# Ends of two mixture-of-experts stages taken in single token blocks, and the loads of the stages after them moved past the block end

## Chip, cores and metric

The kernel is one program on one core of one Trainium2 chip. The metric is the device time of one execution in microseconds (us); less is better. PE is TensorE, PEld its weight load, DVE VectorE, ACT ScalarE, POOL GpSimd, SP the sync engine that only issues transfers. A name with q (SPq, POOLq) is that engine's sequencer.

## What is computed

The reference runs four layers on x of shape 2 x 1024 x 256, T = 2048 rows in all. Two parts matter here, layer 1's top-2 experts with the attention block that follows, and layer 2's experts that choose tokens with the attention that follows:

```python
# layer 1, feed-forward: every token goes to its 2 best of 8 experts
for eid in range(e):
    w = jnp.sum(jnp.where(idx == eid, vals, jnp.zeros((), x.dtype)), axis=-1)
    h = jax.nn.gelu(x_flat @ w1[eid].T, approximate=False)
    y = h @ w2[eid].T
    out = out + w[:, None] * y
# layer 2, attention block: self attention, context attention, feed-forward, each under a layer norm
y = layernorm(y + sa, g1, beta1)
y = layernorm(y + ca, g2, beta2)
y = layernorm(y + ff, g3, beta3)
# layer 2, feed-forward: each of 8 experts takes its 1024 best tokens
h = jax.nn.silu(jnp.einsum('ecd,edh->ech', routed, w1)) * jnp.einsum('ecd,edh->ech', routed, w3)
routed_out = jnp.einsum('ech,ehd->ecd', h, w2).reshape(-1, dim)
out = jnp.zeros_like(xt).at[token_idx].add(routed_out)
# layer 3, attention: queries from the rows, keys and values from the context of 77 rows
out = jnp.einsum('bhqk,bhkd->bhqd', weights, vh)
```

## The kernel before, in words

The rows x stay on chip as 16 token blocks of 128 rows (`k.x`). `program` runs stages one after another; each stage is one `nc.Block()`, in which each engine has its own list of instructions, written out by hand, and only semaphores order the engines. A block ends when every engine has reached its end (each passes a DRAIN there); then `Semaphores.clear` clears the stage's semaphores and all engines meet once more (L790, L791). Only then does the next stage's first instruction start.

**`top2_experts` (tiles with t_).** 23 tiles (TILES) of 256 token slots, sorted by expert. For tile j PE turns the gathered rows, multiplies them by w1 (layer1), and, one tile later, by w2 (layer2); a product of float32 precision is three matmuls (`split_matmul`, L798 to L800). layer2 puts two token blocks of 128 (u = 0, 1) side by side in one PSUM bank and signals `y_psum` once for both. DVE scales both with the gates in one instruction (`scaled`, L1395), and POOL adds them to the DRAM tensor `t_total` with two indirect DMAs (`add`, L1276). POOL starts tile j's adds only when tile j-1's have landed, since two adds to one row must not be in flight together. At the end SP waits for all adds and issues eight loads of the sum back into x (L1261), signalled by `k.x_back`; they need not have landed at the block's end.

**`transformer_block` (tb_).** SP loads `tb_after`, eight columns `tb_turned`, then `tb_affine`, the context rows and the weights. PE begins with 28 filler matmuls (`keep_busy`, L1419) that compute nothing and stand there for the clock; then it waits for the first normalised rows. DVE takes the first statistics (`first_moments`, L2127) once `x_back[0]` has been signalled.

**`choice_experts` (ch_).** 16 groups s (8 experts x 2 turns) of four token blocks. PE's order is layer1(s), turn(s+1), layer2(s-1); each layer2 is 48 matmuls in two halves of two token blocks, each half in its own bank. layer2 waits at its start for all four parts of `ch_hid_lo`. DVE copies each half (`take_output`, L2832) and POOL adds it to `ch_total` with two indirect DMAs (`add`, L2645). At the end SP waits until all adds have landed.

**`narrow_attention` with tag L3_ (tiles L_).** SP loads x back from `ch_total` in four groups, the first two ahead of the weights and biases of keys and values. PE's list is keys (L3452), values (L3459), the turned rows of group 0 (L3444), queries (L3481), ... and, once keys and values are placed, the first scores (L3493). DVE's list is: statistics and normalising of token blocks 0 to 7 (L3305, L3662), the keys into their block-diagonal place (`L_kbd`, L3695), statistics of blocks 8 to 15, values (L3670), four more blocks normalised, values again, the mask (L3714), and then `take` of the first scores (L3723).

The lines that begin DVE's list in that attention:

```python
statistics(range(0, NT // 2))
normalise(range(0, NT // 2))
constants(dve)
...
dve.wait_ge(kv_loaded, 64)
dve.wait_ge(keys_psum, 1)
```

## Time and profile before

| what | value |
|---|---|
| runs of the kernel before | 1691.48, 1693.34, 1696.11 us; median 1693.34 |
| the profiled execution | 1693.98 us, its span 1692.2 us |
| busy share of the span | PE 85%, PEld 71%, DVE 65%, ACT 45%, POOL 38% |
| top-2 stage ends, transformer block begins | 789 us into the span |
| choice stage ends, last attention begins | 1458 us into the span |
| granted TensorE clock, mean | 0.93 |

Times are counted from the span's start. In a timeline row the first number is the start and the second the length of a run of equal instructions; the bracket at the end says how long the engine had sat idle and what released it. The order in which instructions stand is shown below as the built programs have it; no time is in those rows.

### The profile page before, as it was taken

To read this page: it belongs to the slowest core of one execution; us is meant where nothing else is said; L and a number is where in the kernel's file an instruction comes from. 1 tells how busy PE (TensorE), PEld (TensorE's weight loads), DVE (VectorE), ACT (ScalarE), POOL (GpSimd) and SP (SyncE) were. 2 spreads that over 40 slices of the span, in tenths; PEclk is the share of its full clock that TensorE was granted. 3 is DMA by queue.
4 is the path that set the end of the run, shared out by engine and by line. 5 is a ranking of instruction groups with operands and counts; after the bars stand their busy time and mean duration, and the time that the engine had idled before them with its cause. 6 is when DMAs were issued, how large, how long until landed. Compare 5 with 4: busy or idle time off the path is not lost. (4 is left out here: it accounts for less than half of the span.)

```text
span 1692.2 us, 25636 instructions
## 1 busy us (share of the span) xinstructions
PE 1432.9 (85%) x9588; PEld 1203.8 (71%) x9597; DVE 1102.1 (65%) x2351; ACT 759.6 (45%) x1305; POOL 643.5 (38%) x437
## 2 busy tenths in 40 slices
PE   6998769997859999996899997669999999499774
PEld 4886558896449999995677776237888888368632
DVE  7775667987466777763465554585766665477487
ACT  2553645553136676762445333113334443145465
POOL 2451225566024555542132223022665554344200
PEclk9997879999979999997899998888999999799898
DMA  5000000000356777755100000413454443500001
GB/s 188 1 2 5 1 1 1 1 1 1 115 175 203 220 218 220 222 157 109 38 1 1 1 1 0 139 62 105 101 96 99 90 92 46 118 1 2 1 1 50
DMA packets 94177, 122.04 MB, mean 72 GB/s; under 512 B 12300, under 2 KB 79271, under 8 KB 94055
## 3 DMA queue, kind: packets, MB, share of 16 engines
q1 hardware_dynamic: 72935, 91.56, 17.0%
q0 software_dynamic: 21120, 28.85, 9.5%
q8 instruction: 77, 1.26, 0.3%
q14 instruction: 45, 0.37, 0.1%
HBM read 94.95 MB, written 25.43 MB: 71 GB/s over the span
## 5 line engine op out<-in xcount | busy, mean ns | idle before, releaser
L2645 POOL DMA_INDIRECT ch_total<-ch_y,ch_index x64 | 107.7, 1684 | 122.2 <-DVE ch_y L2832 107.3
L1276 POOL DMA_INDIRECT t_total<-t_y,t_index x46 | 99.6, 2166 | 130.2 <-DVE t_y L1395 120.3
L3647 POOL TENSOR_TENSOR L_s<-L_s,L_mx 128x1232 f32<-128x1232 f32 x32 | 76.4, 2389 | 122.8 <-DVE L_mx L3731 122.8
L2769 ACT ACTIVATE ch_silu<-ch_ps 128x512 f32<-128x512 f32 x64 | 38.3, 598 | 170.0 <-PE ch_ps L800 170.0
L798 PE MATMUL ch_ps<-ch_hT_hi,ch_w_hi 128*128 128x512 f32 x256 | 103.9, 406 | 10.6 <-DVE ch_hid L2858 7.3
L798 PE MATMUL t_ps<-t_hT_hi,t_w_hi 128*128 128x256 f32 x368 | 106.3, 289 | 6.0 <-DVE t_w_lo L1383 6.0
L798 PE MATMUL t_ps<-t_w_hi,t_act_hi 128*128 128x256 f32 x368 | 106.0, 288 | 0.0
L799 PE MATMUL t_ps<-t_hT_lo,t_w_hi 128*128 128x256 f32 x368 | 105.4, 286 | 0.0
L800 PE MATMUL t_ps<-t_hT_hi,t_w_lo 128*128 128x256 f32 x368 | 105.3, 286 | 0.0
L800 PE MATMUL t_ps<-t_w_hi,t_act_lo 128*128 128x256 f32 x368 | 104.3, 283 | 0.0
L799 PE MATMUL t_ps<-t_w_lo,t_act_hi 128*128 128x256 f32 x368 | 104.3, 283 | 0.0
L799 PE MATMUL ch_ps<-ch_hT_lo,ch_w_hi 128*128 128x512 f32 x256 | 102.3, 400 | 0.0
L800 PE MATMUL ch_ps<-ch_hT_hi,ch_w_lo 128*128 128x512 f32 x256 | 102.2, 399 | 0.0
L2858 DVE TENSOR_TENSOR ch_hid<-ch_silu,ch_ps 128x512 f32<-128x512 f32 x64 | 43.5, 685 | 77.2 <-ACT ch_silu L2769 75.9
L3515 PEld LDWEIGHTS L_ps<-L_vb,L_pT 128*128 128x128 f32 (+1 forms) x640 | 73.9, 192 | 15.9 <-ACT L_pT L3624 15.9
L3515 PE MATMUL L_ps<-L_vb,L_pT 128*128 128x51 f32 (+2 forms) x640 | 77.6, 278 | 8.1 <-ACT L_pT L3624 8.0
L2635 POOL DMA_INDIRECT ch_hg<-ch_rows,ch_index x64 | 69.9, 1092 | 31.4 <-issue 18.9
L1407 DVE TENSOR_TENSOR t_act_lo<-t_whole,t_act_hi 128x512 fp32r<-128x512 f32 x92 | 61.6, 689 | 25.5 <-ACT t_whole L1369 22.9
L594 POOL TENSOR_TENSOR L_s<-L_s,wk_kb 128x1232 f32<-128x1232 f32 x16 | 45.5, 2846 | 85.3 <-DVE L_s L656 85.3
L798 PEld LDWEIGHTS t_ps<-t_hT_hi,t_w_hi 128*128 128x128 f32 x368 | 71.8, 195 | 6.2 <-issue 6.2
L3723 DVE TENSOR_TENSOR L_s<-L_ps,L_neg 128x616 f32<-128x616 f32 x64 | 48.2, 794 | 41.9 <-PE L_ps L3493 41.9
L1218 POOL DMA_INDIRECT t_hg<-t_rows,t_index x46 | 52.5, 1142 | 58.6 <-DVEq L1704 42.4
(579 smaller groups left out, 4544.0 us busy)
## 6 DMA issues: line engine op xcount, KB each, us to landing
t_w_in<-in_L_ffn_w1T SPq DMA_DIRECT2D x23, 1024.0 KB, 4.9
t_w_in<-in_L_ffn_w2T SPq DMA_DIRECT2D x23, 1024.0 KB, 5.7
ch_w_in<-in_L_ffn_w SPq DMA_DIRECT2D x24, 512.0 KB, 4.2
x<-in_x SPq DMA_DIRECT2D x4, 512.0 KB, 4.9
t_total<-x SPq DMA_DIRECT2D x1, 2048.0 KB
t_rows<-t2d_h SPq DMA_DIRECT2D x1, 2048.0 KB
x<-t_total SPq DMA_DIRECT2D x8, 256.0 KB, 4.6
tb_w<-in_L_xattn_w SPq DMA_DIRECT2D x2, 1024.0 KB, 10.0
```

The lines of the kernel that those rows point to most:

```text
L594: nc.gpsimd.tensor_tensor(flat, flat, kb[:, n // BT, :], ALU.add).then_inc(biased, 1)
L798: nc.tensor.matmul(out, sh, mh, start=start, stop=False)
L799: nc.tensor.matmul(out, sh, ml, start=False, stop=False)
L800: return nc.tensor.matmul(out, sl, mh, start=False, stop=stop)
L1218: nc.gpsimd.indirect_dma_start(out=hg[:, j % 3, u, :], out_offset=None, in_=rows, in_offset=bass.IndirectOffsetOnAxis(ap=index[:, 2 * j + ...
L1276: nc.gpsimd.indirect_dma_start(out=total, out_offset=bass.IndirectOffsetOnAxis(ap=index[:, 2 * j + u:2 * j + u + 1], axis=0), in_=y[:, j % ...
L1407: nc.vector.tensor_tensor(act_lo[:, j % 2, 2 * q:2 * q + 2, :], whole[:, q % 2], act_hi[:, j % 2, 2 * q:2 * q + 2, :].bitcast(F32), ALU.su ...
L2635: nc.gpsimd.indirect_dma_start(out=hg[:, s % 3, u, :], out_offset=None, in_=rows, in_offset=at(s, u)).then_inc(gathered[s % 3], 16)
L2645: nc.gpsimd.indirect_dma_start(out=total, out_offset=at(s, u), in_=y[:, s % 2, u, :], in_offset=None, compute_op=ALU.add).then_inc(added[s ...
L3515: ins = nc.tensor.matmul(ps_o()[:, h0 * HEAD:h1 * HEAD], pT[0:rows, n % 2, f, :], vb[0:rows, b, f, 0:(h1 - h0) * HEAD], start=(f == 0), st ...
L3647: nc.gpsimd.tensor_tensor(s[:, n % G], s[:, n % G], spread(mx[:, n % G, :], 2, [P, H, KEYS]), ALU.subtract).then_inc(shifted, 1)
L3723: nc.vector.tensor_tensor(s[:, n % G, c * 8:(c + 1) * 8, :].rearrange("p (j i) n -> p j i n", i=2), ps[:, 0:BANDS, c * 2 * KEYS:(c + 1) * ...
```

## The change

Four things, of which all arithmetic but the grouping is left as it was:

1. In the last two tiles of `top2_experts` and the last two groups of `choice_experts` the outputs leave in smaller pieces: PE signals after each token block, each block has PSUM space of its own, DVE copies or scales 256 columns at a time, POOL adds each as it comes. In the last choice group PE computes three of the four blocks of layer2(14) ahead of layer1(15) instead of all four behind it.
2. layer2 of every choice group waits for each part of `hid_lo` where it is used, not for all four at the start.
3. SP's waits for the adds leave the ends of both expert stages. They stand now in the next stage: in `transformer_block` behind `tb_after` and the eight `tb_turned` columns, with the eight loads of x behind them; in the last attention behind six loads of weights and biases, ahead of all loads of x. The tiles that the adds read (`index`, `y`) and the semaphores `added` live on into the next stage (`hold`).
4. In the last attention DVE places the keys first, and takes blocks 0 to 3 and 4 to 7 as two rounds of statistics and normalising instead of one of eight blocks.

The core of the diff. SP's end of `top2_experts` goes, and stands in `transformer_block` behind the loads of `after` and `turned`:

```diff
-            for n in range(2):
-                sp.wait_ge(added[n], 32 * len(range(n, TILES, 2)))
-            for m in range(BT // DUO):
-                for b in range(B):
-                    ts = slice(b * BT + m * DUO, b * BT + (m + 1) * DUO)
-                    sp.dma_start(k.x[:, ts, :], total[0:T, :].rearrange("(t p) d -> p t d", p=P)[:, ts, :]
-                                 ).then_inc(k.x_back[m], 16)
...
+            for n in range(2):
+                sp.wait_ge(k.added[n], 32 * len(range(n, TILES, 2)))
+            for m in range(BT // DUO):
+                for b in range(B):
+                    ts = slice(b * BT + m * DUO, b * BT + (m + 1) * DUO)
+                    sp.dma_start(k.x[:, ts, :], k.top2_total[0:T, :].rearrange("(t p) d -> p t d", p=P)[:, ts, :]
+                                 ).then_inc(k.x_back[m], 16)
```

`top2_experts`, DVE's scaling in the last two tiles:

```diff
+                for u in range(2):
+                    dve.wait_ge(y_psum, outputs_to(j, u))
+                    nc.vector.tensor_scalar(y[:, j % 2, u, :], ps_y(j, u), slot_gate[:, 2 * j + u:2 * j + u + 1], None, ALU.mult
+                                            ).then_inc(y_ready, 1)
```

`choice_experts`, the pieces, layer2's waits, PE's order and SP's end:

```diff
+        def pieces(s):
+            if s < BEFORE:
+                return ((0, 2), (2, 4))
+            return ((0, 2), (2, 3), (3, 4)) if s == BEFORE else ((0, 1), (1, 2), (2, 3), (3, 4))
...
-            for n in range(2):
-                sp.wait_ge(added[n], 16 * G * (GROUPS // 2))
...
-                pe.wait_ge(hid_lo_ready, (s + 1) * CHC)
...
+                            pe.wait_ge(hid_lo_ready, s * CHC + c + 1)
...
+                if s == LAST:
+                    layer2(BEFORE, (0, 1))
                 layer1(s)
                 if s + 1 < GROUPS:
                     turn(s + 1)
-                if s:
-                    layer2(s - 1)
-            layer2(GROUPS - 1)
+                if s == LAST:
+                    layer2(BEFORE, (2,))
+                elif s:
+                    layer2(s - 1, (0, 1))
+            layer2(LAST, range(4))
```

`narrow_attention`, SP and then DVE (`a.after` holds the adds' semaphores in the last attention and is empty in the first):

```diff
-            rows(0)
-            rows(1)
+            if not a.after:
+                rows(0)
+                rows(1)
...
+            for sem_added, count in a.after:
+                sp.wait_ge(sem_added, count)
+            if a.after:
+                rows(0)
+                rows(1)
             rows(2)
...
+            if a.after:
+                keys_taken()
+                for g in range(2):
+                    statistics(range(g * G, (g + 1) * G))
+                    normalise(range(g * G, (g + 1) * G))
+            else:
+                statistics(range(0, NT // 2))
+                normalise(range(0, NT // 2))
```

SP where `top2_experts` ends and `transformer_block` begins, before (L1261 is the load of x; the two branches are the block's end and the next one's start):

```order
166 L1261 DMA x<-t_total 128x2x256 x8
167 L1183 UNCONDITIONAL_BRANCH
168 L1800 UNCONDITIONAL_BRANCH
169 L1802 DMA tb_after<-in_after 128x128
170 L1805 DMA tb_turned<-in_L_xattn_g 128x1 x2
171 L1805 DMA tb_turned<-in_L_xattn_beta 128x1 x2
```

and in the changed kernel:

```order
166 L1183 UNCONDITIONAL_BRANCH
167 L1809 UNCONDITIONAL_BRANCH
168 L1811 DMA tb_after<-in_after 128x128
169 L1814 DMA tb_turned<-in_L_xattn_g 128x1 x2
170 L1814 DMA tb_turned<-in_L_xattn_beta 128x1 x2
171 L1814 DMA tb_turned<-in_L_xattn_g 128x1 x2
172 L1814 DMA tb_turned<-in_L_xattn_beta 128x1 x2
173 L1821 DMA x<-t_total 128x2x256 x8
```

The eight loads of x have moved from ahead of the block's end to behind it and behind nine other loads.

DVE at the start of the last attention, before (`L_st` is a block's statistics, `L_h` the normalised rows, `L_kbd` the placed keys; the rows left out are the short chain that makes the inverse roots):

```order
1499 L3305 BN_STATS L_st<-x 128x6 x8
...
1510 L823 SCALAR_TENSOR_TENSOR L_rstd<-L_tmp,L_rstd 128x8
1511 L3662 TENSOR_SCALAR L_h<-x,L_mv,L_rstd 128x256 x8
1512 L3695 TENSOR_SCALAR L_kbd<-L_ps,L_cols,own_key 128x2x77 x4
1513 L3305 BN_STATS L_st<-x 128x6 x8
```

and in the changed kernel:

```order
1501 L3731 TENSOR_SCALAR L_kbd<-L_ps,L_cols,own_key 128x2x77 x4
1502 L3343 BN_STATS L_st<-x 128x6 x4
...
1513 L823 SCALAR_TENSOR_TENSOR L_rstd<-L_tmp,L_rstd 128x4
1514 L3706 TENSOR_SCALAR L_h<-x,L_mv,L_rstd 128x256 x4
1515 L3343 BN_STATS L_st<-x 128x6 x4
...
1527 L3706 TENSOR_SCALAR L_h<-x,L_mv,L_rstd 128x256 x4
1528 L3343 BN_STATS L_st<-x 128x6 x8
```

The keys stand first, and the chain of short instructions stands twice instead of once ahead of the third row of statistics.

## Rows read from the trace of the kernel before

**Rows 1.** Timeline of POOL, last adds of the top-2 stage (start, length, engine, line).
```profile
773.89 1.56 POOL L1276 DMA_INDIRECT t_total<-t_y,t_index  x1 [0.30 <-issue]
778.35 1.55 POOL L1276 DMA_INDIRECT t_total<-t_y,t_index  x1 [2.90 <-DMA t_total<-t_y,t_index]
780.21 1.56 POOL L1276 DMA_INDIRECT t_total<-t_y,t_index  x1 [0.30 <-issue]
```
**Rows 2.** Timeline of SP around the end of the top-2 stage.
```profile
783.91 3.96 SPq L1261 DMA_DIRECT2D x<-t_total  x8
788.97 0.35 SPq L1802 DMA_DIRECT2D tb_after<-in_after  x1
...
793.38 0.43 SPq L1808 DMA_DIRECT2D tb_affine<-in_L_xattn_g  x1
```
**Rows 3.** Block end of the top-2 stage, by line: ns min/median/max, start us.
```profile
L1183 POOLq DRAIN  x1: 9050/9050/9050, 778.6 to 778.6; - x1
```
**Rows 4.** Block end of the choice stage, by line.
```profile
L2554 POOLq DRAIN  x1: 10357/10357/10357, 1447.0 to 1447.0; - x1
...
L2554 SPq DRAIN  x1: 7/7/7, 1455.9 to 1455.9; - x1
```
**Rows 5.** Timeline of DVE across the end of the top-2 stage.
```profile
776.82 0.69 DVE L1395 TENSOR_TENSOR t_y<-t_ps,t_slot_gate 128x512 f32<-128x512 f32 x1 [5.06 <-PE t_ps L800]
789.01 1.08 DVE L2127 BATCH_NORM_STATS2 tb_st<-x 128x6 f32<-128x256 f32 x3 [11.50 <-PEq L791]
```
**Rows 6.** Tile x from 783 to 790 us: issue to landing of its eight loads.
```profile
DMA to landing us min/median/max: 2.7/4.6/5.4
```
**Rows 7.** Timeline of PE at the start of the transformer block.
```profile
789.01 5.15 PE L1419 MATMUL tb_ps<-ident 128*128 128x256 bf16 x28 [12.23 <-PEq L791]
...
795.49 1.58 PE L1854 MATMUL tb_ps<-tb_y0T 128*128 128x128 f32 x8 [0.18 <-ACTq L1991]
...
804.36 2.60 PE L1854 MATMUL tb_ps<-tb_y0T 128*128 128x128 f32 x8
```
**Rows 8.** Windows: length, busy PE, PEld, DVE, ACT, POOL, granted clock, DMA share, GB/s.
```profile
783.00:789.00 6.00, 0.00 (x0) 0.02 (x1) 0.00 (x0) 0.00 (x0) 0.00 (x0) 0.50 0.70 193
794.00:796.00 2.00, 1.82 (x16) 1.48 (x15) 0.00 (x0) 1.40 (x3) 0.00 (x0) 1.00 0.41 111
```
**Rows 9.** Timeline of PE, first and last matmul of the last two layer2 (96).
```profile
1434.78 0.28 PE L798 MATMUL ch_ps<-ch_w_hi,ch_hid_hi 128*128 128x256 f32 x1
...
1445.97 0.28 PE L800 MATMUL ch_ps<-ch_w_hi,ch_hid_lo 128*128 128x256 f32 x1
```
**Rows 10.** Timelines of DVE and POOL at the end of the choice stage.
```profile
1436.22 1.46 DVE L2824 TENSOR_TENSOR ch_hid_lo<-ch_hid,ch_hid_hi 128x512 fp32r<-128x512 f32 x2
...
1451.83 1.56 POOL L2645 DMA_INDIRECT ch_total<-ch_y,ch_index  x1 [0.30 <-issue]
```
**Rows 11.** Timeline of SP at the start of the last attention.
```profile
1459.40 0.50 SPq L3408 DMA_DIRECT2D L_wk<-in_L_xattn_Wk  x1
...
1461.07 0.43 SPq L3411 DMA_DIRECT2D L_cols<-in_L_xattn_bv  x1
...
1462.53 0.98 SPq L3402 DMA_DIRECT2D x<-ch_total  x2
```
**Rows 12.** Timeline of PE at the start of the last attention: the keys.
```profile
1465.91 2.42 PE L3452 MATMUL L_ps<-ctxT,L_wk 128*128 128x154 f32 x8 [19.67 <-DMA L_cols<-in_L_xattn_bv]
```
**Rows 13.** Timeline of DVE at the start of the last attention.
```profile
1464.03 2.71 DVE L3305 BATCH_NORM_STATS2 L_st<-x 128x6 f32<-128x256 f32 x8 [17.06 <-DMA x<-ch_total]
...
1469.27 2.67 DVE L3662 TENSOR_SCALAR L_h<-x,L_mv,L_rstd 128x256 f32<-128x256 f32 x8
1471.86 1.46 DVE L3695 TENSOR_SCALAR L_kbd<-L_ps,L_cols,own_key 128x154 f32<-128x154 f32 x4
1473.25 2.69 DVE L3305 BATCH_NORM_STATS2 L_st<-x 128x6 f32<-128x256 f32 x8
...
1482.17 1.51 DVE L3723 TENSOR_TENSOR L_s<-L_ps,L_neg 128x616 f32<-128x616 f32 x2 [0.33 <-PE L_ps L3493]
```

More of the change, by code:

```diff
@@ L1238, in ps_t, with ps_y, ps_both, outputs_to @@
             return ps[:, 4 + j % 2, :].rearrange("p (c n) -> p c n", c=KC)
[L1240 removed]
+        LAST_TWO = TILES - 2
+        def ps_y(j, u):
+            bank, at = (6 + j % 2, u) if j < LAST_TWO or u == 0 else (4 + j % 2, 0)
+            return ps[:, bank, at * D:(at + 1) * D]
+        def ps_both(j):
             return ps[:, 6 + j % 2, :].rearrange("p (u n) -> p u n", u=2)
[L1243 removed]
+        def outputs_to(j, u):
+            return j + 1 if j < LAST_TWO else LAST_TWO + 2 * (j - LAST_TWO) + u + 1
+        added = k.added
         w1_hi_ready, w1_lo_ready = sem("w1_hi_ready"), sem("w1_lo_ready")
@@ L1271, in add @@
             def add(j):
-                pool.wait_ge(y_ready, j + 1)
-                if j:
-                    pool.wait_ge(added[(j - 1) % 2], 32 * ((j - 1) // 2 + 1))
                 for u in range(2):
+                    pool.wait_ge(y_ready, outputs_to(j, u))
+                    if j and u == 0:
+                        pool.wait_ge(added[(j - 1) % 2], 32 * ((j - 1) // 2 + 1))
                     nc.gpsimd.indirect_dma_start(
@@ L2607, in choice_experts @@
         gathered = [sem(f"gathered{n}") for n in range(3)]
-        added = [sem(f"added{n}") for n in range(2)]
+        added = k.added
         routed_ready, hT_psum, hT_hi_ready, hT_lo_ready = sem("routed"), sem("hT_psum"), sem("hT_hi"), sem("hT_lo")
@@ L2638, in add @@
             def add(s):
-                for half in range(2):
-                    pool.wait_ge(y_ready, 2 * s + half + 1)
-                    if s and s % TURNS == 0 and not half:
-                        for n in range(2):
-                            pool.wait_ge(added[n], 16 * G * (s // 2))
-                    for u in (2 * half, 2 * half + 1):
+                for n, (first, last) in enumerate(pieces(s)):
+                    pool.wait_ge(y_ready, outputs_to(s, n))
+                    if s and s % TURNS == 0 and not n:
+                        for m in range(2):
+                            pool.wait_ge(added[m], 16 * G * (s // 2))
+                    for u in range(first, last):
                         nc.gpsimd.indirect_dma_start(out=total, out_offset=at(s, u), in_=y[:, s % 2, u, :], in_offset=None,
@@ L2826, in hid_rest, with take_output @@
                                         ).then_inc(hid_lo_ready, 1)
-            def take_output(s, half):
-                dve.wait_ge(y_psum, 2 * s + half + 1)
+            def take_output(s, n):
+                first, last = pieces(s)[n]
+                dve.wait_ge(y_psum, outputs_to(s, n))
                 if s >= 2:
                     dve.wait_ge(added[s % 2], 16 * G * (s // 2))
-                nc.vector.tensor_copy(y[:, s % 2, 2 * half:2 * half + 2, :], ps_y(half)).then_inc(y_ready, 1)
+                nc.vector.tensor_copy(y[:, s % 2, first:last, :], ps_y(s, first, last)).then_inc(y_ready, 1)
             dve.wait_ge(value_ready, 1)
@@ L2852, in _ @@
                     table(e)
+                if s == LAST:
+                    for n in range(2):
+                        take_output(BEFORE, n)
                 for c in range(CHC):
@@ L2869, in _ @@
                         weight_lo(e, m)
-                if s:
-                    for half in range(2):
-                        take_output(s - 1, half)
+                if s == LAST:
+                    take_output(BEFORE, 2)
+                elif s:
+                    for n in range(2):
+                        take_output(s - 1, n)
                 if 1 <= s <= down.STEPS:
                     down.step(dve, s - 1)
+            for n in range(4):
+                take_output(LAST, n)
             down.finished(dve)
-            for half in range(2):
-                take_output(GROUPS - 1, half)
 IH = 704
@@ L3690, in _ @@
                 dve.wait_ge(own_key_ready, 2)
-            dve.wait_ge(kv_loaded, 64)
-            dve.wait_ge(keys_psum, 1)
-            for c in range(HC16):
-                for part in range(2):
-                    nc.vector.tensor_scalar(kbd[:, c, :, part, :],
-                                            ps[:, 0, c * BK:(c + 1) * BK].rearrange("p (b n) -> p b n", b=B),
-                                            cols[:, 0, c:c + 1], k.own_key[:, part:part + 1], ALU.add, ALU.mult
-                                            ).then_inc(kbd_ready, 1)
+            if not a.after:
+                keys_taken()
             statistics(range(NT // 2, NT))
@@ L3806, in program, with hold @@
         wide_keys = WideKeys(nc, k, wide)
+        held = ctx.enter_context(ExitStack())
+        def hold(tag, slots, rows):
+            k.held = {"index": held.enter_context(nc.sbuf_tensor(tag + "index", slots, I32)),
+                      "y": held.enter_context(nc.sbuf_tensor(tag + "y", rows, F32))}
+            k.added = [handed(f"{tag}added{n}") for n in range(2)]
         stages = [
```

75 lines of the change are left out of this document (47 added, 28 removed).

## The prediction
> **What bounds the kernel at the two places.** I read four views, in this order. First the timelines of all engines around the two stage ends. In the top-2 stage PE's work is over at 776.7 us, and the next stage starts only at 789.0; in between stand POOL's last adds [rows 1], SP's eight loads of x [rows 2] and the meeting of the engines. In the choice stage PE's work ends at 1446.2 and the next stage starts at 1458.4, behind a queue of POOL's adds [rows 9, 10]. So some 24 us are idle on PE, and this is what the change reaches for.
>
> Second, the lines that end the two blocks, because the question is what the block's end waits for when SP no longer waits. POOL's DRAIN answers it. In the choice stage it starts at 1447.0 and lasts 10.36 us, to 1457.4 [rows 4]. POOL's last add was issued at 1451.83 and its instruction was over at 1453.39 [rows 10]; SP had seen all adds landed and stood at its own DRAIN at 1455.9 [rows 4]. Nobody but POOL was still missing, yet the block ended 1.5 us later, with POOL's DRAIN. In the top-2 stage the same DRAIN runs from 778.6 to 787.6 [rows 3], 5.8 us past the end of the last add instruction at 781.77 [rows 1], and hides there behind SP's issues, which end at 787.87 [rows 2]. **POOL's DRAIN does not end while its adds are in flight**, and the change leaves it where it is. I read this as the block's end waiting for the adds with or without SP.
>
> Third, the first instructions of each next stage: what they wait for and what stands ahead of it on SP [rows 2, 5, 6, 11 to 13]. Fourth, the granted clock around PE's idle stretch [rows 8].
>
> **Top-2 end: the last add is issued 2.4 us earlier.** The last tile's second token block leaves PE where both did, just before 776.82 [rows 5]. DVE's instruction over half the columns I take as 0.40 us for 0.69 [rows 5] (bounds 0.35, half, and 0.69); it ends at 777.2, and POOL follows 0.3 later. POOL must also have issued the block before it, and that waits for the tile before to land: its last add went out at 773.89 and released POOL at 778.35 [rows 1], at most 4.46 later. It goes out 0.3 earlier or more now, only after half a DVE instruction; at the latest the pair starts at 776.2 and the last add at 778.05. I take 777.8 (bounds 777.5 and 778.3) against 780.21 [rows 1].
>
> **From last add to next stage: 6.6 us.** In the choice stage the next stage starts at 1458.43, 6.60 us after the start of the last add at 1451.83 [rows 10], with DRAIN deciding and no other transfer running. The top-2 stage had 8.8 with the loads of x in flight [rows 1, 5]; these are gone now. So 6.6 it is, and the transformer block's engines start at 784.4 instead of 789.0. Bounds: 1.56 + 1.1 = 2.7 if DRAIN holds nothing (a rival below), 8.8 as before.
>
> **Loads of x: 4.9 us later.** `tb_after` and the eight columns go first. Their issue takes 793.38 - 788.97 = 4.41 us [rows 2]. The adds have long landed, so the first load of x is issued at 784.4 + 4.4 = 788.8, against 783.91. Statistics need the first two loads. Issue of the second is 0.5 later, landing takes 2.7 to 4.6 us [rows 6], and in the kernel before both had landed by 789.0, 4.6 at most after the second's issue. The first loads of an empty queue lie at the short end; with 3.0 the statistics begin at 792.3 (792.0 to 793.9), against 789.01 [rows 5]. **+3.3 us.** Everything in this stage follows from the first statistics, and the later loads of x come 1.4 us apart or less with 9 us of slack, so the shift passes on whole. `tb_affine` and the weights are issued at the same times as before within 0.6 us, so nothing is won there.
>
> **The clock: +1.4 us.** PE's 28 fillers last 5.15 us and today end where the first rows arrive; the clock is at 0.50 (1.2 GHz) after PE's idle stretch and 1.00 (2.4 GHz) when the real work begins [rows 7, 8]. In the change they run from 784.4 to 789.6, and the first rows come at 794.0 + 3.3 = 797.3. PE sits idle for 7.7 us between, and it had fallen to 0.50 in the 6 us of idleness from 783 [rows 8]. The first scores then cost 2.60 instead of 1.58 us, as the same eight matmuls did at the low clock [rows 7], +1.0; with six fillers and the turning at half rate I take +1.4 (bounds 0 and 3). The Trainium skill speaks against this order too ("TensorE: Matmul & The Clock Gate", Why this matters for your kernels): no idle gaps between bursts of matmuls, or the clock drops. By the rule the warm-up buys nothing; were the clock to survive the gap, the sum would be 1.4 less.
>
> **Choice end: the last add is issued 1.8 us earlier.** PE's pitch in layer2 is (1445.97 - 1434.78) / 95 = 0.118 us [rows 9]. 36 matmuls move ahead of layer1(15), 4.24 us, so the last `hid_lo` is ready not at 1437.68 [rows 10] but at 1441.92, and only then does DVE copy the last block of group 14 (0.40), at 1442.3. POOL then has five adds left, at 1.56 + 0.30 each, and PE gives them faster than that (12 matmuls, 1.4 us). The last one starts at 1442.6 + 4 x 1.865 = 1450.05, against 1451.83: -1.8. Bounds: -1.2 if PE stalls for `hid_lo` a little, -2.2. The next stage starts at 1450.05 + 6.6 = 1456.65 instead of 1458.43. The 240 added waits on `hid_lo` are met when they come up, except in the last group; I cost them at nothing, because PE's waits on `y_ready` amid the same stream leave the pitch at 0.118 [rows 9].
>
> **Last attention: that gain is spent, and 1.45 us more.** DVE now begins with the keys. The last of their loads is issued 1461.07 - 1459.40 = 1.67 us after the first [rows 11]. Before, they stood behind 1 MB of x, and PE was released by them at 1465.91 [rows 12], 4.8 us after the issue; alone I take 2.5 (bounds 2.4 and 4.8). PE starts the keys 4.25 after the stage's start, DVE has them 2.5 later [rows 12] and places them in 1.4 [rows 13]; statistics begin at +8.25, at 1464.9. Before they began at 1464.03. x is not late: issued at +3.13 [rows 11], landed about 4 to 5 later. Then blocks 0 to 7 cost 2.71 + 2.53 + 2.67 with one chain of 2.53 [rows 13]; in two rounds the chain comes twice, 2.25 for four blocks: 2 x 4.9 = 9.8. From there to the first `take` it is 1482.17 - 1473.25 = 8.92 [rows 13], unchanged. Sum: 1456.65 + 8.25 + 9.8 + 8.92 = 1483.6, against 1482.17. DVE is busy without a gap all this way, and PE's first scores wait for it [rows 13], so the 16 blocks follow. **+1.45 us** (bounds -1.0 and +3.8). That h of blocks 0 to 3 comes earlier helps nobody: scores wait for DVE's keys and values anyway.
>
> **Sum.** +3.3 +1.4 +1.45 = +6.15 us. The profiled execution took 1693.98, 0.64 above the median, so the median goes from 1693.34 to 1699.5.
>
> The skill's "DMA: Bandwidth & Descriptors" (Anatomy of one DMA) gives a GpSimd transfer 2.0 us plus its bytes at 436 GB/s, an estimate of 2.3 us for these 128 KB. Here an add released its waiter after up to 4.5 us; by the page both stages would start some 1.4 us earlier, and the forecast would be near 1697.
>
> **Rivals.** One: **DRAIN holds nothing** and its length only shows SP's wait (for: in the top-2 stage the block ended with SP; against: rows 4). Then the transformer block starts at 777.8 + 2.7 = 780.5, x is issued at 784.9 and statistics begin at 788.4, -0.6; the clock's +1.4 stays. The last attention starts at 1452.75; x waits for the adds' landing at 1453.9 and is there by 1458.9, keys by 1461.0; first take at 1479.7, -2.4. Sum -1.6: 1691.7, not slower. It decides if the next stage begins under 4 us after the last add. Chance 0.12.
>
> Two: **the same chain, but smaller**: the clock's cost vanishes among PE's later waits, or the last attention absorbs its delay in PE's and ACT's queues. Sum +1 to +5, say 1696.5. For it: PE is at 0.50 again soon after anyway, in the second scores [rows 7]. Chance 0.28.
>
> Three: **the added waits break PE's stream** in choice, where PE has no slack. At 0.05 us each, 240 waits give +12: 1711. Against: rows 9. Chance 0.05.
>
> **The numbers.** The forecast has 0.50. A measurement can tell about 0.3%, 5.1 us, from no change. Slower than that: forecast 0.50 and rival three 0.05, together 0.55. Within it: rival two, and rival one: 0.40. Faster by more, for what I don't see: 0.05; even rival one doesn't reach it. The range runs from rival one's side, 1693, to the forecast with its upper bounds (clock +3, attention +3), 1705.
>
> **What would show it.** Right: POOL's DRAIN still ends both blocks 5.5 us after the start of the last add; the transformer block starts near 784 and its first statistics near 792, released by x; fillers end 7 us before the first real matmul, whose clock is 0.50; the last attention starts near 1456.7 relative to an unshifted stage, with its first take about 27 us later. Wrong: a stage that starts under 4 us after the last add, a take less than 25 us after the stage's start, or layer2 matmuls slower than 0.118 us apart.

## The result, and the profile after

| | before | after |
|---|---|---|
| median of the runs (11 each, same chip), us | 1693.18 | 1703.86 |
| ratio, 95% interval | | 1.0057 (1.0043 to 1.0072) |
| span of the profiled execution, us | 1692.2 | 1704.2 |

Each ratio here and below is to executions of the kernel before made beside it on one chip, and leaves out the rare execution with a lower clock throughout (one of experiment 1's, 1826.89 us), which the medians keep. Medians of different experiments are in part from different chips.

The change made the kernel slower by 0.57%, about 10 us, where 6.15 were forecast; 1703.86 lies near the top of the stated range of 1693 to 1705. The profiled execution of the changed kernel, 1705.99 us, was 2.1 above its median, so the stages below show 12 us more and not 10. The stages around it can be cut out of both traces, from POOL's last barrier instruction of one to that of the next. This view of windows gives their length first, then busy time of PE, PEld, DVE, ACT and POOL, granted clock, DMA share and GB/s; the rows are top-2, transformer block, choice and last attention, and a stretch of 47 us from 28 us after the last attention's start. First of the kernel before:

```profile
438.66:788.68 350.02, 319.05 (x2526) 300.32 (x2529) 224.38 (x289) 202.94 (x263) 154.11 (x100) 0.96 0.64 190
788.68:1068.87 280.19, 233.99 (x1066) 184.85 (x1066) 147.69 (x572) 114.40 (x273) 71.37 (x57) 0.93 0.06 16
1068.87:1458.14 389.27, 345.83 (x2101) 281.29 (x2104) 248.74 (x526) 126.13 (x194) 179.33 (x135) 0.95 0.43 93
1458.14:1599.68 141.54, 120.06 (x932) 95.44 (x932) 90.22 (x190) 61.32 (x112) 47.37 (x34) 0.91 0.10 29
1486.14:1533.14 47.00, 43.01 (x369) 33.47 (x367) 32.01 (x45) 25.50 (x43) 22.70 (x16) 1.00 0.00 1
```

And of the changed one:

```profile
438.68:786.51 347.83, 319.22 (x2526) 300.51 (x2529) 224.98 (x291) 202.85 (x263) 152.84 (x100) 0.96 0.63 188
786.51:1075.79 289.28, 234.94 (x1066) 185.62 (x1066) 148.19 (x572) 114.39 (x273) 71.38 (x57) 0.92 0.07 19
1075.79:1463.50 387.71, 348.09 (x2101) 281.66 (x2104) 249.25 (x529) 126.13 (x194) 179.18 (x135) 0.95 0.42 93
1463.50:1612.38 148.88, 127.95 (x932) 101.74 (x932) 91.87 (x200) 61.51 (x112) 47.37 (x34) 0.88 0.10 27
1491.50:1538.50 47.00, 43.25 (x304) 31.31 (x304) 29.54 (x40) 21.83 (x37) 20.59 (x14) 0.88 0.00 1
```

Both expert stages became shorter, by 2.2 and 1.6 us, and both stages behind them longer, by 9.1 and 7.3. The forecast had -4.6 and +9.3 for the first pair, so +4.7; it came to +6.9. For the second pair it had -1.8 and +3.25, so +1.45; it came to +5.8. The stage behind the last attention, the int8 feed-forward, took 0.7 back.

**Top-2 end and transformer block.** Last add, DRAIN, SP, DVE and PE of the changed kernel, from the timelines and the view by line; the counterparts are [rows 1 to 3, 5, 7].

```profile
776.48 1.56 POOL L1278 DMA_INDIRECT t_total<-held_y,held_index  x1 [2.83 <-DMA t_total<-held_y,held_index]
778.34 1.56 POOL L1278 DMA_INDIRECT t_total<-held_y,held_index  x1 [0.30 <-issue]
```
```profile
L1183 POOLq DRAIN  x1: 8242/8242/8242, 777.6 to 777.6; - x1
```
```profile
786.80 0.35 SPq L1811 DMA_DIRECT2D tb_after<-in_after  x1
...
791.23 3.97 SPq L1821 DMA_DIRECT2D x<-t_total  x8
```
```profile
794.71 0.43 DVE L2143 BATCH_NORM_STATS2 tb_st<-x 128x6 f32<-128x256 f32 x1 [17.14 <-DMA x<-t_total]
```
```profile
786.84 4.57 PE L1428 MATMUL tb_ps<-ident 128*128 128x256 bf16 x28 [9.79 <-PEq L791]
799.69 1.12 PE L1846 MATMUL tb_ps<-ident,tb_y 128*128 128x128 f32 x4 [8.28 <-ACT tb_y L1979]
...
801.88 2.17 PE L1870 MATMUL tb_ps<-tb_y0T 128*128 128x128 f32 x8
```

The last add went out 1.9 us earlier than before, and the next stage began at 786.8, 8.5 us after it and not the 6.6 assumed. No load of x was in flight any more, and still POOL's DRAIN went on until 785.8, 5.9 us past the end of the add's instruction. Then everything is as forecast: 4.4 us of SP's own loads ahead of x, 3.5 us from the first load's issue to the statistics, and PE idle for 8.3 us behind its fillers. A cut of the clock there shows the fillers raise it, the wait run it down, and the first turned rows and scores start at 0.50, which is 1.2 GHz:

```profile
787.00:792.00 5.00, 4.41 (x28) 3.23 (x26) 0.00 (x0) 0.00 (x0) 0.00 (x0) 0.74 0.15 17
792.00:799.60 7.60, 0.00 (x0) 0.00 (x0) 3.41 (x19) 1.05 (x3) 0.00 (x0) 0.79 0.95 298
800.00:802.00 2.00, 2.00 (x11) 1.63 (x10) 0.00 (x0) 1.21 (x3) 0.00 (x0) 0.50 0.93 142
```

Statistics are 5.7 us late, and the stage's end 6.9. The 1.2 between are the clock's as I read them; experiment 9 looks at it directly.

**Choice end and last attention**, beside [rows 4, 10 to 13]:

```profile
1457.21 1.56 POOL L2671 DMA_INDIRECT ch_total<-held_y,held_index  x1 [0.30 <-issue]
```
```profile
L2570 POOLq DRAIN  x1: 8367/8367/8367, 1454.4 to 1454.4; - x1
```
```profile
1470.56 1.47 DVE L3731 TENSOR_SCALAR L_kbd<-L_ps,L_cols,own_key 128x154 f32<-128x154 f32 x4 [16.21 <-PE L_ps L3496]
1471.95 1.39 DVE L3343 BATCH_NORM_STATS2 L_st<-x 128x6 f32<-128x256 f32 x4
...
1491.34 0.80 DVE L3777 TENSOR_TENSOR L_s<-L_ps,L_neg 128x616 f32<-128x616 f32 x1 [0.93 <-PE L_ps L3537]
```
```profile
1489.81 1.41 PE L3537 MATMUL L_ps<-L_kbd,L_qT 32*128 32x154 f32 x16 [3.09 <-issue]
1491.14 6.20 PE L3525 MATMUL L_ps<-L_hT,L_wq_sb 128*128 128x512 f32 x8
...
1512.79 4.07 PE L3559 MATMUL L_ps<-L_vb,L_pT 128*128 128x34 f32 x20 [0.46 <-ACT L_pT L3668]
1516.66 1.95 PE L3546 MATMUL L_ps<-ident,L_s 128*128 128x128 f32 x8
```

The last attention starts at 1463.78, 6.57 after the last add. Statistics begin 8.17 after that, as worked out (8.25), and the first take of scores 27.56 (26.97). The 0.6 between is the first scores, 1.41 us at half clock for 0.81. Two more pieces stand in no term of the sum: the second queries last 6.20 (5.40 before), and from about 1513 PE runs at the low clock again in the middle of its work. PE had been idle for 1.2 us from 1504.6 on and for 0.8 us from 1511.1 on, and before has the same two pauses without a fall. The same piece of work in before (first) and after shows the price; 4.07 for 2.42 us, 1.95 for 1.07 and 1.41 for 0.81 make 3.1 us.

```profile
1502.00:1509.00 7.00, 6.30 (x62) 5.47 (x62) 4.87 (x8) 4.64 (x9) 2.94 (x2) 1.00 0.00 0
```
```profile
1512.00:1519.00 7.00, 6.54 (x38) 5.95 (x42) 2.82 (x4) 2.76 (x5) 2.93 (x2) 0.59 0.00 0
```

So my theory for the experiments: SP's order ahead of x, and a start that is 8.5 and not 6.6 us behind the last add, make the first 6.9; keys first and two rounds on DVE, and a lower clock, make the rest. What stayed unclear was what POOL's DRAIN waits for, and whether the clock's fall is chance.

A stage is compared by its own length below, since the stages ahead of top-2, which no kernel here touches, ended anywhere from 430.4 to 441.9 us in these profiles.

### The profile page after: what moved, and what is told of

Its sections match the earlier page's. It is cut to its first block and busy times, and to the rows that moved or that the text cites. A ratio compares the mean times of both kernels' runs of the same rounds, so it can differ in the third digit from the quotient of the medians.

```text
span 1704.2 us, 25671 instructions
## 1 busy us (share of the span) xinstructions
PE 1443.0 (85%) x9588; PEld 1210.2 (71%) x9597; DVE 1106.1 (65%) x2366; ACT 759.8 (45%) x1305; POOL 642.1 (38%) x437
## 5 line engine op out<-in xcount | busy, mean ns | idle before, releaser
L2671 POOL DMA_INDIRECT ch_total<-held_y,held_index x64 | 107.6, 1681 | 120.8 <-DVE held_y L2865 103.1
L1278 POOL DMA_INDIRECT t_total<-held_y,held_index x46 | 98.1, 2133 | 129.5 <-DVE held_y L1399 114.9
L2661 POOL DMA_INDIRECT ch_hg<-ch_rows,held_index x64 | 69.9, 1092 | 31.4 <-issue 18.9
L1219 POOL DMA_INDIRECT t_hg<-t_rows,held_index x46 | 52.8, 1147 | 58.6 <-DVEq L1713 42.4
```

Of the source, the lines that this page charges most:

```text
L1219: nc.gpsimd.indirect_dma_start(out=hg[:, j % 3, u, :], out_offset=None, in_=rows, in_offset=bass.IndirectOffsetOnAxis(ap=index[:, 2 * j + ...
L1278: nc.gpsimd.indirect_dma_start(out=total, out_offset=bass.IndirectOffsetOnAxis(ap=index[:, 2 * j + u:2 * j + u + 1], axis=0), in_=y[:, j % ...
L2661: nc.gpsimd.indirect_dma_start(out=hg[:, s % 3, u, :], out_offset=None, in_=rows, in_offset=at(s, u)).then_inc(gathered[s % 3], 16)
L2671: nc.gpsimd.indirect_dma_start(out=total, out_offset=at(s, u), in_=y[:, s % 2, u, :], in_offset=None, compute_op=ALU.add).then_inc(added[s ...
```

## Experiments

**1. Loads of x first.** In the changed kernel, the transformer block's SP:
```diff
+            [the wait for k.added and the eight loads of x]
             sp.dma_start(after[:], i["after128"])...
             [eight columns]
-            [the wait for k.added and the eight loads of x]
```


> The changed kernel with one thing different: in the transformer block SP waits for the adds and issues the eight loads of x first, the after-table and the eight columns behind them. Theory (SP's order ahead of x costs the wait, not the transfer): the block still starts at 786.8, the first statistics begin about 4.4 us earlier, near 790.3 instead of 794.71, and the run is 4.4 us shorter than the changed kernel, 5.6 if the clock's part goes too (PE's idle gap shrinks from 8.3 to some 4 us). Rival (the loads of x are slow because columns and x share queues and descriptors, wherever they stand): statistics begin under 2 us earlier, and the columns, now last, delay the first turned rows, so the run stays within 1.5 us of the changed kernel.

Measured: ratio to before 1.0046 (1.0024 to 1.0068), median 1701.48. The transformer block took 285.87 us, 3.4 less than changed. Its first load was issued at 784.81 and statistics began at 789.14, so 4.33 after the stage's start for 7.91: 3.6 us won, not 4.4, as the two loads took 4.3 us from issue where they had taken 3.5 behind the columns. The timed gain, 0.0011 or 1.9 us, is less than the traces have, and the interval overlaps that of the changed kernel. The clock's part stayed: PE was idle for 4.70 us and the first scores lasted 2.45. SP's order is the larger part of the 5.7; the rest is that loads issued behind the barrier bring the statistics 12.8 us after the last add, and loads issued ahead of it 8.8 [rows 1, 5].

**2. Top-2 end as before.** SP's wait and the loads of x back in top-2; the rest as changed.


> The changed kernel with SP's wait and the eight loads of x put back at the end of the top-2 stage; adds in single blocks and the last attention stay as changed. Theory: the loads are issued when the adds have landed, about 782, so 2 us before the 783.9 of the kernel before; statistics begin near 787.3 against 794.71, PE's fillers reach the first rows and the first scores cost 1.58 again; the run is 7.4 + 1.3 = 8.7 us shorter than the changed kernel, near 1695. Rival (the block's end waits for whatever is in flight, x too, and moves later by what the loads gain): statistics begin no earlier than 789, and the run is at most 7 us shorter.

Measured: 1.0011 (0.9991 to 1.0031), median 1695.57. Last add at 775.54, first load of x at 779.28, statistics at 784.38 without a wait for x, first scores 1.58 us. Top-2 plus block took 629.3 us against 637.1 in the changed kernel, 7.8 less. The block's end waits for SP's eight issues again, so the statistics come 8.84 after the last add, as in [rows 1, 5]. The theory had 8.7; the ratios give 7.8 (1.0057 less 1.0011), and the two intervals do not overlap.

**3. Last attention as before, without the wait at choice's end.**
```diff
+            for sem_added, count in a.after: sp.wait_ge(sem_added, count)
+            rows(0); rows(1)
             [weights]
-            [the wait, rows(0), rows(1)]
...
-            keys_taken(); two rounds of statistics and normalise
+            statistics(8 blocks); normalise(8 blocks); ...; keys_taken()
```


> The changed kernel with the last attention's order undone: SP waits for the adds at the stage's start, then loads x ahead of the weights, and DVE does statistics of eight blocks, their scaling, then the keys. The wait at the end of the choice stage stays away. Theory (the chain on DVE, keys first and two rounds, costs 3.8 us to the first scores taken, and the lower clock in the stage 3.5 more): first scores are taken 23.7 us after the stage's start against 27.6, and the run is 3.8 us shorter than the changed kernel by the chain alone, 7.3 if the clock is also as before. Rival (the last attention was longer by the clock's chance fall alone): the first take moves, but PE's queue makes it up and the run is under 2 us shorter.

Measured: 1.0035 (1.0022 to 1.0048), median 1699.29. The stage took 142.53 us, 6.35 less than changed, its first take came 24.2 after its start, and the clock did not fall:
```profile
1463.34:1605.87 142.53, 121.77 (x932) 96.42 (x932) 90.22 (x190) 61.33 (x112) 47.36 (x34) 0.90 0.10 29
1491.34:1538.34 47.00, 43.01 (x361) 32.89 (x359) 31.41 (x44) 25.69 (x44) 23.23 (x16) 0.99 0.01 1
```
Both halves of the theory show in this profile. The timed runs give 3.7 us (1.0057 less 1.0035), the chain's part alone, with intervals that overlap by a little. The first scores took 1.41 us here too, and the second queries 6.0, so these two are not the keys-first order's own.

**4. POOL waits for its own adds.** Behind the last add of each expert stage: `for n in range(2): pool.wait_ge(added[n], ...)`.


> The changed kernel with POOL itself waiting for its adds' semaphores behind the last add of both expert stages, ahead of its DRAIN. Theory one (DRAIN lasts as long as the adds are in flight, and their semaphores tell the same): both next stages start within 0.5 us of where they do, 786.8 and 1463.8, DRAIN is short, and the run is unchanged. Rival (DRAIN goes on 1.7 to 3.8 us beyond the landing, as SP's sight of it in the kernel before suggests, by its own polling): with the wait, DRAIN begins when nothing is in flight and is over at once, the transformer block starts near 783.5 and the last attention 1.5 us earlier, and the run is some 4 to 5 us shorter.

Measured: 1.0066 (1.0042 to 1.0091), median 1706.39. Both expectations fell, by when the stages start; in time it can't be told from the changed kernel:
```profile
L1183 POOLq DRAIN  x1: 4546/4546/4546, 779.0 to 779.0; - x1
```
```profile
L2572 POOLq DRAIN  x1: 3980/3980/3980, 1459.5 to 1459.5; - x1
```
The last adds were issued at 775.09 and 1455.45, and POOL, having seen them landed, stood at its DRAIN 3.9 and 4.05 us later. No add was in flight then, and DRAIN still took 4.55 and 3.98 us. Both next stages started later, 9.4 and 9.0 us after the last add instead of 8.5 and 6.6. **DRAIN has some 4 us of work of its own**; my reading of its length as "adds in flight" was wrong.

**5. Single blocks alone.** Experiments 2 and 3 together.


> Only the first part of the change: adds in single blocks at both ends; SP's wait and the loads of x stand again at the end of the top-2 stage, and the last attention loads x first, with DVE's order of before. Theory (parts add up: last adds 2 us earlier in top-2 and 1.8 in choice, each passing on whole): statistics of the transformer block begin 2 us after the time of the kernel before minus 4, so some 2 us earlier relative to the top-2 stage's own start, the choice stage is 1.6 us shorter, the last attention as long as before, and the run is 3.5 us shorter than the kernel before: 1690.5, ratio 0.998. Rival (the earlier adds are worth nothing because the stage ends are set by something else, or moving 36 matmuls ahead of the first layer costs what it gains): ratio 1.000, within 1 us.

Measured: 0.9991 (0.9974 to 1.0008), median 1691.32. Top-2 347.93, block 279.07, choice 388.80, last attention 142.75: 2.5 us less than before over the four stages. The 2.1 of top-2 are there; choice gave 0.5 of 1.6. No difference is shown by the timed runs. So the smaller pieces are not what made the changed kernel slower.

**6. A DRAIN in between.** Experiment 5, with `nc.gpsimd.drain()` on POOL ahead of the last two tiles' and the last two groups' adds.


> As the run with single blocks only, and POOL executes one more DRAIN amid each expert stage: ahead of the last two tiles' adds in top-2, ahead of the last two groups' adds in choice. The run with POOL's waits showed DRAIN to last 4.5 and 4.0 us although nothing was in flight any more. Theory one (DRAIN's 4 us are work on all that POOL issued since its last DRAIN, reclaiming entries): the DRAIN at the block's end is much shorter, under 2 us past the last add's instruction in the choice stage, and the last attention starts 2 to 3 us earlier. Theory two (DRAIN waits for what is in flight and has a fixed price of about 4 us beside it): it ends 4.0 us after the last add's instruction as ever, and the added DRAINs either hide in POOL's idle time or cost up to 4 us each.

Measured: 0.9994 (0.9968 to 1.0020), median 1694.43. The last DRAINs of both stages:
```profile
L1183 POOLq DRAIN  x1: 5469/5469/5469, 781.9 to 781.9; - x1
```
```profile
L2572 POOLq DRAIN  x1: 7015/7015/7015, 1452.6 to 1452.6; - x1
```
They end at 787.3 and 1459.7, 3.8 and 4.2 us after the start of the last adds (783.50, 1455.47), which is when adds had landed in experiment 4. Theory one holds in kind: with four or eight adds since the last DRAIN there is no work of its own left to see. Its sizes did not come: in choice DRAIN ends 2.6 us past the add's instruction, not under 2, and the last attention starts 5.3 us after the last add for 6.6. In top-2 nothing is gained, as SP's eight issues decide there (8.7), and the added DRAIN delays the last adds by 2.0 us. The 0.7 us by which choice's last add is later than in experiment 5 lie within what this stage varies by itself (below, at "The last adds").

**7. Fillers in the last attention.** Changed kernel, `keep_busy` of 18 ahead of the keys, 18 behind the values, 24 ahead of the first scores.


> The changed kernel with fillers on PE in the last attention: 18 before the keys, 18 between the values and the first turned rows, 24 between the placement and the first scores. Theory (3.5 us of the stage's 7.3 are the clock: the low clock through queries(1) and its fall again some 50 us into the stage): PE's granted clock is 1.00 from the turned rows on, the first scores last 0.81 us, queries(1) 3.7 to 4.5, no fall near 50 us, and the stage from start to end is 3 to 4 us shorter than the 148.9 of the changed kernel. Rival (DVE's chain sets the stage, the clock only fills PE's idle time): the first take moves 0.6 us, the stage's end under 1.5 us.

One run, 1701.73. The turned rows and queries(0) ran at full clock (3.70 for 4.95 us), but the last fillers ended 3.0 us before the first scores, which took 1.41 us again, and queries(1) 5.98. First take 27.34, stage 145.58, with no fall later. The 3.3 us less than the changed kernel are not theirs for sure: experiment 4, with the same last attention and no fillers, had 146.10.

**8. One round on DVE**, SP's order as changed.


> The changed kernel, but DVE does statistics and scaling of blocks 0 to 7 in one round behind the keys, not in two rounds of four; SP's order stays as changed. Theory (two rounds repeat the chain of small instructions, 2.2 us): the first take comes 2.2 us earlier after the stage's start, 25.3 instead of 27.56, while the first turned rows come 2.7 us later on PE, and the stage is about 2 us shorter. Rival (PE's queue behind the turned rows sets the first scores): queries(0) then end later than DVE and the first take comes 26.5 or later.

One run, 1698.95. First take at 26.88, not 25.3. Statistics of eight blocks needed the second load of x too and began at 9.37 for 8.17; and PE set the first scores, behind queries(0) at the low clock. Stage 145.23 us. The rival's sign, 26.5 or later, is there. The second round costs 2.2 us on DVE and buys back 1.2 by starting earlier.

**9. Fillers across the gap.** Changed kernel, 98 fillers for 28 at the start of the transformer block.


> The changed kernel with 98 fillers instead of 28 at the start of the transformer block, so that PE is busy until about the first turned rows. Theory (the idle gap of 8.3 us between fillers and first rows costs 1.3 us by the lower clock): the first turned rows start no later after the statistics (4.98 us), the clock there is 1.00, the first scores last 1.58 us against 2.17 and the mask and the turned probabilities come 1.0 to 1.3 us earlier after the statistics; the stage is 1.3 us shorter than the 289.3 of the changed kernel. Rival (the clock falls again anyway in the wait behind the first scores): the second scores last 2.6 us as in the changed kernel and under 0.7 us is won. In the last attention, which is the changed one, a second look at the clock: 148.9 us if it falls again 50 us into the stage, 146 if not.

One run, 1699.70.
```profile
791.43 0.66 PE L1846 MATMUL tb_ps<-ident,tb_y 128*128 128x128 f32 x4 [0.69 <-ACT tb_y L1979]
...
792.92 1.58 PE L1870 MATMUL tb_ps<-tb_y0T 128*128 128x128 f32 x8 [0.18 <-ACTq L2007]
```
From the statistics to the second scores it was 15.1 us, 16.6 in the changed kernel and 15.35 in [rows 5, 7]: the clock's price is 1.3 to 1.5 us there. In the stage's length 0.9 us are left (288.35), which shows nothing by itself, since the same block with 28 fillers behind the late start took 287.8 to 291.9 us in five profiles. In one of these (experiment 4) the second scores came 14.7 us after the statistics in spite of the gap. In its last attention the clock fell as in the changed kernel, 149.64 us and 0.85:
```profile
1483.55:1530.55 47.00, 43.48 (x302) 32.35 (x300) 28.89 (x40) 21.80 (x36) 20.59 (x14) 0.85 0.01 1
```

**10. A version to beat both.** Experiment 5, two of x's loads at top-2's end, two at the block's start and four behind the columns; the extra DRAINs earlier, where POOL idles over 5 us.
```diff
 # top-2, SP: wait for added, then
-            for m in range(BT // DUO): [loads of x]
+            for m in (0,): [loads of x]
 # transformer block, SP
+            for m in (1,): [loads of x]
             [tb_after, columns]
+            for m in range(2, BT // DUO): [loads of x]
 # POOL
+                if j == LAST_TWO - 1: nc.gpsimd.drain()     # top-2
+                if s == BEFORE: nc.gpsimd.drain()           # choice
```


> A version meant to beat both: adds in single blocks at both ends and the last attention of before; POOL's extra DRAIN stands where POOL has over 5 us of idle time (top-2: ahead of the adds of the third last tile; choice: ahead of those of the third last group); SP issues two loads of x at the end of the top-2 stage, two at the start of the transformer block, and four behind the columns. Theory (the end's DRAIN then lasts only until the last add has landed, 3.9 to 4.1 us after its start, and SP's block end no longer waits for eight issues): the transformer block starts 6.0 us after the last add in place of 8.8 and its statistics 7.7 us after it, the last attention starts 5.2 us after its last add in place of 6.6, and the run is 2.5 us shorter than the run with single blocks only, 4.5 shorter than the kernel before: near 1689, ratio 0.997. Rival (the DRAIN works off all entries since the last one, and six to twelve adds since are enough to make it 4 us long again): the stages start as in the run with single blocks only, 8 and 6.5 us after the last adds, and only some 1 us is won by the split loads.

Measured: **0.9972 (0.9955 to 0.9989)**, median 1688.99.
```profile
776.69 1.56 POOL L1285 DMA_INDIRECT t_total<-held_y,held_index  x1 [0.30 <-issue]
```
```profile
780.25 0.89 SPq L1270 DMA_DIRECT2D x<-t_total  x2
782.24 0.87 SPq L1823 DMA_DIRECT2D x<-t_total  x2
```
The block starts 5.55 us after the last add and its statistics, at 783.56, 6.9 after; the last attention starts 5.4 after its last add at 1445.27.

**11. One DRAIN in the kernel before**, choice stage, ahead of the third last group's adds.


> The kernel before with nothing changed but one more DRAIN of POOL in the choice stage, ahead of the adds of the third last group. Theory (an added DRAIN in idle time shortens the last one to the landing of the adds): the stage ends 4.1 us after the start of the last add in place of 5.55, and the next one starts 5.2 after it in place of 6.60; the run is 1.4 us shorter if nothing is delayed. Rival (the 12 adds issued since make it long again): 5.55 and 6.60 as before.

One run, 1692.61. DRAIN ended at 1455.27, 4.4 after the last add's start at 1450.84 (5.55 in [rows 4, 10]), and the next stage began 5.5 after it for 6.6. One line moves the end by 1.1 us, where ten profiles without it in that stage all have 5.55; in the choice stage's length 0.8 are left, which is not clear of what that stage varies by, and one run shows no time.

**12. The version of 10 without its DRAINs.**


> The version meant to beat both, without its two added DRAINs: adds in single blocks, the loads of x split over the boundary, the last attention of before. Theory (without a DRAIN in between, the one at the block's end lasts 5.9 us past the last add's instruction in top-2 and 4.0 in choice, whatever SP does): the transformer block starts 8.0 to 8.5 us after its last add, its statistics 0 to 0.3 us behind that, nearly as in the run with single blocks only, the last attention starts 6.5 after its last add, and the run is some 2.5 us longer than with the DRAINs: near 1691.5. Rival (the split of the loads was the gain and the DRAINs did nothing): transformer block's start 6 us after the last add, last attention's 5.3, the run within 0.5 us of 1689.

Measured: 0.9990 (0.9975 to 1.0005), median 1689.46. The DRAINs ended 7.2 and 5.5 us after the last adds, and the stages started 8.2 and 6.6 after them, as the theory had it. But over the four stages its profile took 1156.65 us and that of experiment 10 took 1156.66 (before: 1161.02): what the earlier starts gave was lost again, part of it in the block (281.5 us for 279.4). The last add in choice came 1.0 us later with the DRAIN, but profiles that are alike in this stage differ by more, so this is not shown to be the DRAIN's doing. The two intervals overlap. That the DRAINs pay in time is not shown; of the two versions only that of 10 is shown to be faster than before.

## Why the prediction was right or wrong

**The mechanism was right**, and so was the sign: the 24 idle us behind the last adds are hardly touched by taking SP's wait away, since POOL's DRAIN decides, and what the next stages do in the new order costs more than is gained. Undoing the first half (experiment 2) takes 1.0057 to 1.0011, undoing the second (experiment 3) to 1.0035, and undoing both (experiment 5) to 0.9991; only the second of these steps by itself is not clear of the noise. Rival two, the same chain but smaller, had the way right and the size wrong: it came out larger.

**The size was 4 us short, in two terms.** That it still fell into the range is in part luck with the range's edge: the two upper bounds named for 1705, clock 3 and attention 3, give 3.3 + 3 + 3 = 9.3 and so 1702.6. It takes the statistics' bound of 4.9 and the attention's 3.8 as well to reach 1705.

*"So 6.6 it is, and the transformer block's engines start at 784.4."* This was the mis-sized term: 8.46, start at 786.80. I took the choice stage's number over the top-2 stage's own 8.8 and put the difference down to loads of x in flight. But DRAIN ends 5.7 to 5.95 us past the end of the add's instruction in all eleven profiles without an added wait or DRAIN in that stage, whether loads of x are in flight (before, experiments 2 and 5) or not, and 3.99 past it in choice, in all ten. What sets the difference between the two stages was not found. The rest of the chain (4.4 us of SP, 3.5 of landing) was exact, so the +3.3 became +5.7 with the start 2.4 late.

*"DVE is busy without a gap all this way... +1.45."* The chain on DVE was right within 0.1 up to the last of it (8.17 for 8.25, whose own terms 4.25, 2.5 and 1.4 add up to 8.15; two rounds 9.86 for 9.8), and experiment 2, whose first scores ran at full clock, had its first take 26.97 us after the start, the number forecast. What the sum left out is PE's clock in that stage. In the changed order PE gets its first work in pieces: keys and values, 3 us of nothing, four blocks, 3 us of nothing. In the profile it is +0.6 (first scores), +0.8 (second queries) and +3.1 (the later fall), 4.5 together, of which 4.1 are left in the stage's length. I had asked for the clock at the first boundary only. The first two pieces are no mark of the new order: the first scores took 1.41 us in four of seven profiles with x's rows first, and in four of seven with the keys first. The kernel before was profiled with them at 0.81.

Is the later fall chance? In part. Seven profiles with x's rows first had 141.5 to 143.4 us for the stage (mean 142.5) and a granted clock of 0.93 to 1.00 in the 47 us from 28 us on; five with keys first in the changed form had 143.7 to 149.6 (mean 147.5) and 0.85 to 0.96. The order costs 5 us in the mean, where 3.25 were forecast; each execution draws its own part of the fall. A stretch at 0.50 began 49 to 50 us into the stage in four of the five, for 3.4 to 10.2 us, and 46 to 52 us into it in two of the seven, for 3.4 us. The runs of experiments 7 and 8, keys first in a form of their own and without that fall, had 145.6 and 145.2 us. What in the order brings the fall about was not tried.

**The clock at the transformer block, +1.4**: right, 1.2 by the stages and 1.3 to 1.5 by experiment 9, though it is put together otherwise than forecast: the first scores took 2.17 us and not 2.60, and the first turned rows 1.12 where experiment 9 had 0.66. The Trainium skill ("TensorE: Matmul & The Clock Gate", Why this matters for your kernels) says to leave no gaps between bursts of matmuls; the trace agrees, 0.50 in the first turned rows behind a gap of 8.3 us, and 1.00 with the gap filled.

**The last adds**: 778.34 for 777.8. DVE's last output was ready at 777.57; it was the wait for the tile before to land that held the pair until 776.48, 0.3 us past the latest that I had given it (776.2). In choice the last add came 1.54 us earlier for 1.8, and that is a favourable draw. Counted from the stage's start it went out at 380.7 to 383.0 us in the nine profiles with this stage as changed, 381.9 in the mean, against 382.8 before. **The added waits** cost nothing that can be seen (rival three): choice was 387.1 to 389.5 us in these nine profiles, 388.3 in the mean, 389.3 before.

**Rival one** (DRAIN holds nothing) is dead by both traces. But the reason I gave against it, *"POOL's DRAIN does not end while its adds are in flight"*, was only half of it. Experiments 4, 6 and 11 show two parts: the landing, 3.9 to 4.1 us after the issue, and work of its own of 4 to 4.5 us, which is there with no add in flight and gone from sight when POOL has done another DRAIN not long before. How the two overlap (in top-2 5.9 us past the instruction, in choice 4.0) stays open. The trace of before has one more case that speaks against a fixed price of 4 us: the DRAIN that ends the top-2 stage's first block, behind two gathers only, was over at 487.7, 1.9 us past the end of the second.

The rule of the Trainium skill, "DMA: Bandwidth & Descriptors" (Anatomy of one DMA), that I weighed gave these adds 2.3 us, as an estimate; the measured landings are 3.7 to 4.05.

## What to carry to other kernels

Before taking a wait off one engine at a stage's end, find who arrives last without it, in that stage and not in a similar one; and price what stands ahead of the awaited load in the next stage's queue, since loads issued before the barrier landed during it (8.8 us from the last add to the statistics in the kernel before, 12.8 in experiment 1, where they stood first behind it). When an order of work is changed, ask for the clock wherever PE is fed in pieces, not only at the boundary. If POOL has issued many indirect transfers, one DRAIN in its idle time can bring the block's end forward (1.1 us in experiment 11); check that the next stage can use it, for no time gained by that alone is shown here. And before a difference between two traces is read as the change's work, look how far traces of the same code lie apart in that stage.

## What the runs showed of the hardware

- POOL's DRAIN at the end of a block with indirect adds takes 4.0 to 4.5 us with no add in flight; with four to twelve adds since an earlier DRAIN it ends 3.8 to 4.4 us after the last add's start, about when that lands.
- A block of 128 rows of 1 KB, added by an indirect transfer, was seen as landed 3.7 to 4.05 us after the start of its instruction, which itself takes 1.56.
- The same loads of x took 4.3 us from first issue to the statistics on a queue with nothing ahead of them, and 3.5 behind nine small loads.
- The granted clock of PE fell to 0.50 some 49 us into a stage, behind idle times of 1.2 and 0.8 us that other profiles have without a fall. It was 0.85 to 0.96 over 47 us in five profiles with one order of the stage's first 25 us, and 0.93 to 1.00 in seven with the other.
